# Row sums of the second layer's softmax: folding the probabilities' key blocks with accumulating DMAs ahead of the matmuls that sum them

## What is computed

```
q, k = l2norm(q * 16), l2norm(k);  q, k = q * 4, k * 4        # 16 query heads, one k and one v of 64
sim  = einsum('bhid,bjd->bhij', q, k)                          # causal: j <= i
attn = softmax(sim, axis=-1)
out  = einsum('bhij,bjd->bhid', attn, v)                       # then @ Wout.T, a layer norm
```

## Time and profile before

| | |
|---|---|
| median of three runs | 1293.28 us |
| the profiled execution: its own time | 1296.09 us |
| its span, first to last instruction | 1294.2 us |
| mean granted TensorE clock | 0.971 |
| PE busy | 1170.9 us, 90% of the span |
| DVE busy | 883.1 us, 68% |
| ACT busy | 672.5 us, 52% |
| POOL busy | 457.9 us, 35% |
| DMA, mean over the span | 23 GB/s |

### The profile page before, as it was taken

One profiled execution on the slowest core, in us unless ns is written; L12 is line 12 of the kernel. 1 busy time (PEld: TensorE's weight loads), 2 busy tenths in 40 slices (PEclk: granted clock), 3 DMA queues, 4 the chain that ended last, 5 costly groups with the idle time before them and its releaser, 6 DMA issues. The chain is left out here.

```text
span 1294.2 us, 26914 instructions
## 1 busy us (share of the span) xinstructions
PE 1170.9 (90%) x8812; PEld 799.3 (62%) x8812; DVE 883.1 (68%) x2412; ACT 672.5 (52%) x1294; POOL 457.9 (35%) x687
## 2 busy tenths in 40 slices
PE   5999999999999995799399899998999989999896
PEld 3556566566666653689365766657666676766664
DVE  6888888888888865455355766657666576665744
ACT  2666666666667661355164452644527355263540
POOL 4222212222221225543343361634615345253440
PEclk9999999999999996799699999999999999999999
DMA  2310001000000005222000000000000000000000
GB/s 63 103 25 17 18 18 25 17 17 18 20 23 17 17 10 188 65 61 55 15 10 1 9 8 0 16 0 8 8 0 16 0 10 6 0 16 0 9 1 9
DMA packets 34597, 29.78 MB, mean 23 GB/s; under 512 B 5984, under 2 KB 27104, under 8 KB 34528
## 3 DMA queue, kind: packets, MB, share of 16 engines
q1 hardware_dynamic: 32224, 24.22, 6.7%
q0 software_dynamic: 2304, 4.72, 1.6%
HBM read 13.72 MB, written 6.82 MB: 16 GB/s over the span
## 5 line engine op out<-in xcount | busy, mean ns | idle before, releaser
L1295 ACT ACTIVATE arena<-ring_a 128x384 f32<-128x384 f32 (+1 forms) x512 | 252.6, 550 | 139.8 <-PE ring_a L477 139.8
L1440 ACT ACTIVATE arena<-ring_a 128x1024 f32<-128x1024 f32 x128 | 131.7, 1029 | 156.9 <-PE ring_a L477 156.9
L1058 POOL TENSOR_SCALAR_AFFINE_SELECT arena<-arena 128x512 f32<-128x512 f32 x128 | 81.9, 640 | 356.2 <-ACT arena L1295 356.2
L477 PE MATMUL ring_a<-q_max,rows 128*128 128x384 f32 (+1 forms) x512 | 195.4, 385 | 1.1 <-ACT arena L1295 0.5
L1580 DVE CUSTOM_DVE_ANT_0 arena<-pair,arena 128x384 bf16<-128x384 f32 (+1 forms) x271 | 162.3, 614 | 25.8 <-PE pair L477 22.7
L1202 POOL TENSOR_TENSOR q_len<-q_sum,exponents 128x8 f32<-128x8 f32 x64 | 108.2, 1690 | 141.8 <-DVE q_sum L1869 141.8
L477 PE MATMUL pair<-arena,v_aug 128*64 128x512 f32 (+3 forms) x1024 | 150.2, 438 | 4.0 <-ACT arena L1440 3.5
L477 PE MATMUL ring_a<-rows,k_rows 64*128 64x384 f32 (+2 forms) x1152 | 125.1, 339 | 14.8 <-DVE rows L1888 13.8
L477 PE MATMUL ring_a<-arena,v_aug 128*32 128x384 f32 (+1 forms) x1024 | 122.8, 551 | 2.1 <-POOL arena L1058 1.0
L477 PEld LDWEIGHTS pair<-arena,v_aug 128*64 128x64 f32 x1024 | 68.4, 136 | 85.4 <-issue 68.0
L1230 POOL TENSOR_SCALAR_AFFINE_SELECT arena<-arena 128x256 f32<-128x256 f32 x256 | 96.1, 406 | 56.0 <-ACT arena L1440 56.0
(11 more groups left out here) (255 smaller groups left out, 2199.6 us busy)
## 6 DMA issues: line engine op xcount, KB each, us to landing
rows<-k_rows SPq DMA_DIRECT2D x128, 64.0 KB, 2.0
arena<-in_w SPq DMA_DIRECT2D x2, 2048.0 KB, 14.1
slots_y<-arena SPq DMA_DIRECT2D x40, 64.0 KB
x_all<-in_x SPq DMA_DIRECT2D x8, 256.0 KB, 3.5
tokens_x<-xn_all SPq DMA_DIRECT2D x1, 2048.0 KB, 9.5
out<-o_t SPq DMA_DIRECT2D x8, 256.0 KB, 2.3
arena<-tokens_x,tokens_now POOLq DMA_INDIRECT x40, 2.5
wq_sb<-in_wq_t SPq DMA_DIRECT2D x1, 512.0 KB, 4.8
```

The costliest lines, as they stand in the source:

```text
L477: return pe.matmul(out, lhs, rhs, start=start, stop=stop, skip_group_check=True)
L1058: pool.affine_select(out=v, in_=v, compare_op=ALU.is_ge, fill=0.0, base=0, pattern=[[0, HG], [1 if late else -1, P]], channel_multiplier=- ...
L1295: act.activation(probs[:, t % NT, h, 0:many], A.slot(("cols", c))[:, 0:many], ACT.Exp).then_inc(A.free.sem, A.free.add(1))
L1440: act.activation(dst, src, ACT.Exp).then_inc(ring.free.sem, ring.free.add(1))
```

## The change

The row sums need each column's sum over all keys, and addition can come before the matmul. After `values1(n)` has read a pair's probabilities, DMAs that accumulate add later key blocks onto the first: block 1 onto columns 128 to 512 of block 0 (`fold1`, 128 partitions x 2 heads x 384 floats, 384 KB), block 3 onto the last 128 columns of block 2 (`fold3`, 128 KB), and then block 2 onto the last 256 columns of block 0 (`fold2`, 256 KB). Pairs 0 to 3 get all three, pairs 4 and 5 the first two, pairs 6 and 7 none. `sums1(0)` and `sums1(1)` are then 4 matmuls of 512 columns, `sums1(2)` 8 matmuls (512 and 256 columns), `sums1(3)` stays.

POOL issues these DMAs, in iteration n between `q_length(n + 1)` and the masks of pair n: `fold_last(n - 3)`, which waits until fold1 and fold3 of that pair have landed, then `fold_first(n - 2)`. PE runs `sums1` in iterations 4, 6 and 7, each behind a wait for the DMAs of its two pairs. The exponentials have six buffers in place of four, two of them in a new tensor `late`; `q_hi` and `q_lo` move from `rows` to a new tensor `q_parts`; `late` and `q_parts` lie where `sel` and `rows` of layer 1 lay.

```
-QB, PB = 3, 4
+QB, PB = 3, 6
+N_FOLD, N_FOLD_ALL = 6, 4
...
+        def probs_of(n, j):
+
+            at, many, step, skip = ((1536, 512, 512, 0), (512, 384, 512, 0), (0, 256, 256, 0), (512, 128, 512, 384))[j]
+            return probs1[n % PB][:, at:at + 2 * step].rearrange("p (c t) -> p c t", c=2)[:, :, skip:skip + many]
...
@@ sums1(m), TensorE
-                    for j in range(NT):
+                    if m < N_FOLD_ALL // 2:
+                        pe.wait_ge(s["fold2"].sem, s["fold2"].at(b, 32 * (m + 1)))
+                    elif m < N_FOLD // 2:
+                        for name in ("fold1", "fold3"):
+                            pe.wait_ge(s[name].sem, s[name].at(b, 32 * (m + 1)))
+                    for j in (0,) if m < N_FOLD_ALL // 2 else (0, 2) if m < N_FOLD // 2 else range(NT):
...
                     if n:
                         values1(n - 1)
-                        if n % 2 == 0:
-                            sums1(n // 2 - 1)
+                        if n in (4, 6, 7):
+                            sums1((4, 6, 7).index(n))
...
@@ attend, GpSimd
+                def fold(name, dst, src):
+
+                    pool.dma_start(dst, src, accum_op=ALU.add).then_inc(s[name].sem, s[name].add(16))
+
+                def fold_first(n):
+
+                    pool.wait_ge(s["o_full"].sem, s["O"].filled(b, ("o", n)))
+                    for name in ("fold1", "fold3"):
+                        if n:
+                            pool.wait_ge(s[name].sem, s[name].at(b, 16 * n))
+                    apart(pool)
+                    fold("fold1", probs_of(n, 0)[:, :, P:T], probs_of(n, 1))
+                    fold("fold3", probs_of(n, 2)[:, :, P:2 * P], probs_of(n, 3))
+
+                def fold_last(n):
+
+                    for name in ("fold1", "fold3"):
+                        pool.wait_ge(s[name].sem, s[name].at(b, 16 * (n + 1)))
+                    if n:
+                        pool.wait_ge(s["fold2"].sem, s["fold2"].at(b, 16 * n))
+                    apart(pool)
+                    fold("fold2", probs_of(n, 0)[:, :, 2 * P:T], probs_of(n, 2))
...
                 for n in range(NP):
                     if n + 2 < NP:
                         q_length(s, n + 1, b)
-                    p = probs1[:, n % PB]
+                    if 0 <= n - 3 < N_FOLD_ALL:
+                        fold_last(n - 3)
+                    if 0 <= n - 2 < N_FOLD:
+                        fold_first(n - 2)
+                    p = probs1[n % PB]
...
@@ exp_of(n, third), ScalarE
-                        act.wait_ge(s["pv"].sem, s["pv"].at(b, max(n // 2 - 1, 0)))
+                        act.wait_ge(s["pv"].sem, s["pv"].at(b, 1 if n >= PB else 0))
```

More of the change, by code:

```diff
@@ L96 @@
              e_full=10, e_free=9, own=18, var=1, veps=1, rstd=1,
-             sums=6, lens=6, q_lo=8, h1=3, masked=24, pv=4, g_free=2, inverted=1, fin=1, stored=16)
+             sums=6, lens=6, q_lo=8, h1=3, masked=24, pv=4, g_free=2, inverted=1, fin=1, stored=16,
+             fold1=16 * N_FOLD, fold3=16 * N_FOLD, fold2=16 * N_FOLD_ALL)
 CREDITED = dict(q_lo=1, q_free=1, o_free=1, l_free=1, s_free=1, m_free=1, w_free=1, e_free=1, g_free=1, sums=1, h1=1, r_free=1, added=1, stored=1, pv=1,
@@ L286, in two_layers @@
         rows2 = sb("rows2", [P, 2, HG])
-        sel = sb("sel", [P, G, 4, HG, 4, D0], F32R)
         rev_e = sb("rev_e", [P, NT, NE])
@@ L309, in two_layers @@
         q_max = sb("q_max", [P, 2, T], F32R)
-        rows = sb("rows", [P, H0, T], F32R)
         v_aug = sb("v_aug", [P, NT, H0, 32])
@@ L323, in two_layers @@
         q_sum, q_len, q_rn = sb("q_sum", [P, H1]), sb("q_len", [P, H1]), sb("q_rn", [P, H1])
+        with nc.sbuf_tensor("sel", [P, G, 4, HG, 4, D0], F32R) as sel, nc.sbuf_tensor("rows", [P, H0, T], F32R) as rows:
+            pass
+        q_parts = sb("q_parts", [P, 2 * QB, T], F32R)
+        late = sb("late", [P, 2, 2560])
         probs = arena[:, 0:NT * HG * T].rearrange("p (q h t) -> p q h t", q=NT, h=HG)
@@ L348, in two_layers @@
         tile_steps, tile_rows = parts[:, :, 0, :], parts[:, :, 1, :]
-        probs1 = arena[:, 0:10240].rearrange("p (n t) -> p n t", n=PB)
+        probs1 = [arena[:, n * 2560:n * 2560 + 2560] for n in range(4)] + [late[:, n] for n in range(2)]
+        def probs_of(n, j):
+            at, many, step, skip = ((1536, 512, 512, 0), (512, 384, 512, 0), (0, 256, 256, 0), (512, 128, 512, 384))[j]
+            return probs1[n % PB][:, at:at + 2 * step].rearrange("p (c t) -> p c t", c=2)[:, :, skip:skip + many]
         o1 = arena[:, 10240:14336].rearrange("p (n t) -> p n t", n=NP)
@@ L357, in two_layers @@
         k_nat = k_nat_sb[:].rearrange("p (i r d) -> p i r d", i=NT, r=2)
-        q_hi, q_lo = rows[:, 0:QB, :], rows[:, QB:2 * QB, :]
+        q_hi, q_lo = q_parts[:, 0:QB, :], q_parts[:, QB:2 * QB, :]
         kf, kn = (arena[:, at:at + 256].rearrange("p (i d) -> p i d", i=NT) for at in (15360, 15616))
@@ L807, in p_of @@
                     at += c * (256 if j == 2 else 512)
-                    return probs1[:, n % PB, at:at + many]
+                    return probs1[n % PB][:, at:at + many]
                 def values1(n):
@@ L1215, in attend @@
                     SR[name].restart()
+                def fold(name, dst, src):
[15 more added lines that the diff above has]
+                    fold("fold2", probs_of(n, 0)[:, :, 2 * P:T], probs_of(n, 2))
+                for name in ("fold1", "fold3", "fold2"):
+                    s[name].restart()
                 for n in range(NP):
@@ L1434, in exp_of @@
                     if third == 0:
-                        act.wait_ge(s["pv"].sem, s["pv"].at(b, max(n // 2 - 1, 0)))
-                    dst, src = probs1[:, n % PB, at:at + many], ring.slot(("probs", n, third))[:]
+                        act.wait_ge(s["pv"].sem, s["pv"].at(b, 1 if n >= PB else 0))
+                    dst, src = probs1[n % PB][:, at:at + many], ring.slot(("probs", n, third))[:]
                     if third == 1:
```

## The result

The changed kernel takes 1444.22 us (median of 4 runs, 1441.34 to 1446.01) against 1293.44 us before in the same comparison: a ratio of 1.116, 95% interval 1.1135 to 1.1188. That is 151 us slower, 18.8 us in each of the eight batches. The forecast was 1404 us, 110 us slower, with a range of 1290 to 1525.

A forecast was written before the change was run, and what follows sets the result against it. PE was taken to set the pace (74.9 of 80 us a batch). Waits of 17.5 us behind POOL's issues and fold landings, less 3.66 saved, made 13.8 a batch, 110 in eight: 1404 us from the median, range 1290 to 1525.

The forecast's parts named there:

- What it removes: PE's sums1: fewer streamed columns save 3.66 us a batch, 29 us in 8 batches.
- Cost of an issue: POOL's 16 DMA issues a batch: 1.33 us each, from its indirect issue of 1.03 plus 0.30 between two.
- The upper bound of 2.36 (issue by runs): Rival at POOL: issue time grows with runs, 256 against 128, 2.36 us an issue; 1500 us, chance 0.19.
- the lower one (as SP's): Rival at POOL: issues as cheap as SP's direct ones, 0.7 us with gap; 1327 us, chance 0.15.
- Landing: Folds' DMAs: 1.5 us after the issue plus bytes at 185 KB per us; fold2 alone lands 2.88 us after issue ends.
- the ends of 132 and 265: Fold rates in KB per us: 265 as a plain copy, 132 if the destination moves too; 132 gives 1453 us.
- rule of two source reads: Skill's claim for reducing DMAs: about half the copy rate, so 132 KB per us and about +160 us instead of +110.
- The Trainium skill's fit: Fold landing by the skill's SWDGE estimate: fold2 lands 2.6 us from issue, and the sum would be about +60.
- The chain: PE behind POOL's in-order queue and the folds: seven waits of 17.5 us less 3.66 saved, 13.8 us a batch.
- The sixth: Iteration 6: sums1(1) waits 3.42 us for fold2 of pair 3, which waits for that pair's fold1 and fold3.
- The clock: the step that was missing: PE in layer 2: granted clock stays at 1.00, as through waits of 0.5 us; waits of 3 were not shown.
- The other side's bound: Rival that issues are nearly free: at best 8 us saved, 1285 us, as fold2(1) stands behind q_length(5); faster 0.09, no change 0.06.

The follow-up runs named there:

- The kernel without folds: The changed kernel without its 16 folds a batch and PE's waits for them, sums1 kept short (later key blocks left out): 1265.79 us, ratio 0.979.
- the 512-run DMAs: Against the changed kernel: one DMA folds two pairs (pairs 4 and 5 fold1 only), no fold2, masks first, sums later, sums1(2) last: 1274.39 us, ratio 0.986.
- the scratch folds: The changed kernel with its 16 folds between parts of a spare tensor of zeros, PE not waiting for them, sums1 kept short: 1386.23 us, ratio 1.072.
- the filler: The changed kernel with zero-weight matmuls put where PE waits for masks of pairs 3 and 5 and before sums1(0), (1), (2): 1412.75 us, ratio 1.093.
- 1505: The changed kernel with POOL's folds moved behind the masks of the same iteration, nothing left out: 1505.3 us, ratio 1.165.
- 1392: Kernel of 1505 with sums1(0), (1), (2) moved from iterations 4, 6, 7 to 5, 7 and behind turn_x: 1392.04 us, ratio 1.077.
- 1320: Kernel of 1392 without fold2 (fold1 and fold3 for pairs 0 to 5), sums1(2) last, behind sums1(3): 1320.06 us, ratio 1.021.
- 1293: Against the changed kernel: only fold1 for pairs 0 to 5, behind the masks, sums late, sums1(2) last: 1293.01 us, ratio 1.000.
- 1291: Kernel of the 512-run DMAs, but pairs 4 and 5 get one fold1 and one fold3 for both, issued in iteration 7: 1290.73 us, ratio 0.997.
- 1326: Kernel of 1291 plus a fold2 for pairs 2 and 3 in iteration 7, sums1(1) moved behind sums1(3): 1326.28 us, ratio 1.025.
- The last two runs: Kernel of the 512-run DMAs with pairs 4 and 5 folded together (1290.73 us), then that with a fold2 for pairs 2 and 3 besides (1326.28 us).

## Why the prediction was right, and where it was short

The direction, the mechanism and its places were right; the point was 40 us low of the 151: the low clock alone, which the sum didn't have, is 43.

- *What it removes.* 3.66 us a batch, 29 in all. The kernel without folds shows 26 against its own comparison.
- *Cost of an issue.* Taken as 1.33 us from the indirect row; measured 1.27 by records and 1.41 by the ends around them. The upper bound of 2.36 (issue by runs) is refuted by these and by the 512-run DMAs at 1.38; the lower one (as SP's) by all rows, the shortest of which is 1.19.
- *Landing.* Taken as 1.5 us and 185 KB per us after an issue of 1.33, 4.9 us for fold1 and 4.2 for fold2 from the issue's start; measured 4.5 for a fold1 alone and 3.9 for fold2. Three folds behind one another were sized too short: from the issue of fold2 to the last landing the sum has 7.0 us, and the changed kernel took 7.9 (799.89 to 807.83) and 7.8 (807.83 to 815.58). The rate of 154 lies between the ends of 132 and 265. The Trainium skill's rule of two source reads ("Collectives: The Full Stack") would give 132: the trace is nearer to it than to the copy rate, but not at it. The Trainium skill's fit in "DMA: Bandwidth & Descriptors" (2.0 us plus bytes at 436 GB/s, by estimate 2.9 us for 384 KB) is well below the 4.5 measured.
- *The chain.* Waits foreseen: 1.50, 1.45, 2.44, 3.55, 2.65, 3.42, 2.47, together 17.5. Measured: 0.96, 1.25, 2.66, 3.86, 2.66, 2.04, 2.49, together 15.9, with 0.41 at `project_q(5)` that was not foreseen (DVE's longer step, see the scratch folds). The sixth is short because PE came to it late: `values1(5)` ran 1.7 us longer on the low clock. Without that it would have been 3.70, above the 3.42 foreseen, since the landing was sized too short. That the sum of the waits came so near is in part luck. Less 3.66 this makes 12.7 a batch, 101 us.
- *The clock: the step that was missing.* "The granted clock stays at 1.00" was wrong: it was carried over from waits of 0.5 us (1.06 is PE's longest in that batch before) to waits of 2 to 4. It was at 0.50 three times a batch. Read off against the earlier trace rows: `sums1(0)` takes 1.87 us for 0.92 (789.85 to 791.72), the stretch from there to `values1(4)` 5.51 for 3.64, `values1(5)` 1.66 more, scores(7) 3.60 for 2.68. That is 5.4 us a batch, 43 us, and closes the sum to within 7 us of 151; the filler gave back 31 by experiment (the 1.66 in `values1(5)`, 13 us in eight batches, would have been a wait for fold2 instead). The 7 us left are spread over short gaps that I did not assign.
- *The other side's bound.* A best case of -8 us for this placement was not tried as such. The rows that bounded it (fold2(1) behind `q_length(5)`) were borne out in the changed kernel, where PE waited 3.86 us at that place.

Seven of the eleven expectations of experiments were too low as well: 1386, 1505, 1392, 1320, 1293, 1291 and 1326 us for ranges of my theory that ended at 1345, 1440, 1350, 1300, 1284, 1284 and 1310. The low clock behind waits has a part in five of them (all but 1293 and 1291). That I summed POOL's work by iteration, without the fetch and the folds that stand ahead of one `q_length`, has a part in 1392, 1320 and 1293; a landing sized too short or left out has one in 1505, 1320, 1291 and 1326.

## What to carry to other kernels

An engine that is busy for 44% of the time (POOL's 35 of 80 us) can still have no room: look for what stands behind the new instruction in its queue, and who waits for that. The issue of a DMA had nearly a fixed price here (1.2 to 1.4 us of POOL), so put two transfers into one before making a transfer smaller, ask for the result an iteration later than seems needed, and keep issues out of iterations that are already full; here that turned 151 us of loss into 19 us of gain with the same idea. And price a wait of some microseconds on TensorE above its length: what ran behind it here often ran at half the clock. The last two runs show the limit: larger DMAs land later, and a sum that asks for them too early loses the gain again.

## What the runs showed of the hardware that I had not expected

- TensorE's granted clock fell to half within a wait of 3.9 us that came soon after one of 2.7, and stayed for some 6 us of full work; in the kernel with the scratch folds waits of 2.7 and 3.3 us, with shorter ones ahead of them, were followed by a `values1` of 3.8 and 4.5 us. With two folds a pair a wait of 2.37 us stood behind at least 4 us of full work, and the clock was at 0.50 from 843 to 846 us. But `values1(3)` of the changed kernel, behind 2.66 us of wait, and its `sums1(2)`, behind 2.49, ran at full speed, and so did all behind the wait of 1.76 us with one fold a pair (1.00 from 834 to 842 us, with some 19 us without a wait ahead of it). Matmuls of zeros in the waits kept the clock at 1.00.
- An accumulating DMA from POOL occupies POOL for 1.2 to 1.4 us with 256 runs and 1.4 with 512. From SBUF to SBUF it lands 384 KB in 4.5 us alone and in 4.8 to 5.6 among other folds, and 768 KB in 7.0.
- POOL's `pow` and mask records grew longer beside the issues (masks 1.1 to 1.9 us in the mean for 0.41), since records begin while the instruction in front still holds the engine: the masks of 780.17 begin before the issues end at 781.62. The ends of records gave the cost: `q_length` from 782.07 ends 1.64 us after the masks, as long as it takes before.
- DVE rows beside POOL's issues and masks were up to 2.4 times as long (1.67 us for 0.69). With the folds behind the masks `v_aug` takes 692 ns in the mean again.
